# Attention on one Trainium2 core: a new order for the row-maximum pieces and later places for six products with V

## What is computed

```
h   = layernorm(x)
q, k, v = split(clip(h @ Wqkv.T, -8, 8))          # 512 columns each
q, k = layernorm(q) * q_w + q_b, layernorm(k) * k_w + k_b
scores = q k^T / 4 + alibi(head)                  # 32 heads of 16, causal
x   = x + softmax(scores) @ v @ Wout.T
W_q = sum over 4 of alphas * bases                # 512 x 512
x   = x + layernorm(x) @ W_q.T
```

## Time and profile before

| | |
|---|---|
| median of 3 runs | 701.35 us |
| profiled execution | 701.69 us, its span 700.0 us |
| mean granted TensorE clock | 0.973 of full |
| busy: PE, DVE, ACT, POOL | 673.8, 576.4, 410.5, 313.1 us |
| reductions of maximum pieces (L979) | 608, 358.3 us busy |
| exponentials (L806) | 640, 309.3 us busy |
| products with V (L1161) | 1536 passes, 156.8 us busy |

### The profile page before, as it was taken

The page is one execution under the profiler, slowest core; times in us unless marked ns, Lnnn a source line. Parts: engine busy times, 40 slices in busy tenths (PEclk is TensorE's granted clock), DMA queues, the critical chain, the costliest instruction groups (busy, mean ns, idle before and its releaser), DMA issues.

```text
span 700.0 us, 16007 instructions
## 1 busy us (share of the span) xinstructions
PE 673.8 (96%) x6096; PEld 412.5 (59%) x6096; DVE 576.4 (82%) x990; ACT 410.5 (59%) x855; POOL 313.1 (45%) x403
## 2 busy tenths in 40 slices
PE   3999999998899999999999999999999999899998
PEld 2888888885334554554554455445455543588886
DVE  6899999997999999989999998999999830466664
ACT  5133333232059887888888888888878889222221
POOL 1378666778132642634625523322322535234440
PEclk9999999998569999999999999999999999999999
DMA  8226665868926443343343434334333332245442
GB/s 307 69 68 181 181 181 155 224 174 225 300 89 167 126 134 98 106 128 101 115 124 101 115 109 130 97 113 124 106 113 117 95 92 73 75 135 154 144 131 75
DMA packets 102060, 93.64 MB, mean 134 GB/s; under 512 B 11640, under 2 KB 81912, under 8 KB 101984
## 3 DMA queue, kind: packets, MB, share of 16 engines
q1 hardware_dynamic: 97856, 86.84, 42.4%
q10 hardware_dynamic: 2016, 3.67, 2.0%
q0 software_dynamic: 2112, 2.10, 1.3%
HBM read 57.44 MB, written 33.82 MB: 130 GB/s over the span
## 4 chain that ended last, share of the span: by engine, by line
PE 72%; DVE 16%; issue 7%; DMA 2%; ACT 1%; POOL 1%; SPq 0%; DVEq 0%; POOLq 0%; ACTq 0%
PE ps L1126 23%; PE ps L1161 21%; PE ps L1106 9%; PE ps L1040 5%; PE ps L1041 5%; PE ps L1042 5%; DVE stats L979 4%; DVE qk_stat L924 2%; DVE qk L920 2%; PE ps L1048 2%; PE ps L1102 2%; DVE x_stat L890 1%; DVE xt_lo L883 1%; DMA inv_in<-inv_dram 1%; DVE rest L899 1%
## 5 line engine op out<-in xcount | busy, mean ns | idle before, releaser
L979 DVE TENSOR_REDUCE stats<-ps 128x1 f32<-128x512 f32 (+3 forms) x608 | 358.3, 656 | 31.6 <-PE ps L1106 29.3
L806 ACT ACTIVATE probs<-ps 128x512 f32<-128x512 f32 (+2 forms) x640 | 309.3, 560 | 71.3 <-PE ps L1126 70.9
L1106 PE MATMUL ps<-first_k,first_q 54*128 54x128 bf16 (+3 forms) x1152 | 217.3, 282 | 5.2 <-DVE stats L979 4.7
L1126 PE MATMUL ps<-second_q,second_k 64*128 64x128 bf16 (+4 forms) x1152 | 205.0, 273 | 0.0
L1126 PE MATMUL ps<-first_q,first_k 54*128 54x512 bf16 (+3 forms) x768 | 194.2, 328 | 0.2 <-ACT probs L806 0.2
L1161 PE MATMUL ps<-probs,v_sb 128*32 128x512 f32 (+3 forms) x1536 | 156.8, 496 | 2.0 <-ACT o_sb L837 1.2
L694 POOL TENSOR_SCALAR_AFFINE_SELECT probs<-probs 128x256 f32<-128x256 f32 x256 | 103.0, 408 | 123.7 <-ACT probs L806 116.6
L1126 PEld LDWEIGHTS ps<-first_q,first_k 54*128 54x128 bf16 x768 | 57.7, 94 | 111.1 <-ACT probs L806 108.3
L1106 PEld LDWEIGHTS ps<-first_k,first_q 54*128 54x128 bf16 x1152 | 92.3, 96 | 50.9 <-DVE stats L979 35.9
L1126 PEld LDWEIGHTS ps<-second_q,second_k 50*128 50x128 bf16 (+1 forms) x1152 | 91.8, 95 | 20.9 <-issue 0.6
L1040 PE MATMUL ps<-wqkv_hi,xt_hi 128*128 128x512 f32 x192 | 76.8, 400 | 0.0
(11 more groups left out here) (79 smaller groups left out, 822.7 us busy)
## 6 DMA issues: line engine op xcount, KB each, us to landing
parts_dram<-parts SPq DMA_DIRECT2D x48, 256.0 KB, 4.1
v_dram<-v_ext SPq DMA_DIRECT2D x16, 512.0 KB, 4.0
v_sb<-v_dram SPq DMA_DIRECT2D x16, 512.0 KB, 4.4
o_dram<-o_sb SPq DMA_DIRECT2D x32, 256.0 KB
first_q<-parts_dram SPq DMA_DIRECT2D x96, 64.0 KB
first_k<-parts_dram SPq DMA_DIRECT2D x96, 64.0 KB
second_q<-parts_dram SPq DMA_DIRECT2D x96, 64.0 KB
second_k<-parts_dram SPq DMA_DIRECT2D x96, 64.0 KB
```

The lines of the kernel that those rows point to most:

```text
L806: act.activation(weights, scores, ACT.Exp, scale=SCALE).then_inc(exp_done, 1)
L979: dve.tensor_reduce(to, scores, AX.X, ALU.max).then_inc(max_taken, 1)
L1106: last = pe.matmul(ps[:, bank, r * cols:(r + 1) * cols], first_q[n % STACKS][rows, hp, i * P:(i + 1) * P], first_k[n % STACKS][rows, hp, k ...
L1126: return pe.matmul(ps[:, bank, r * cols + first:r * cols + last], stack_k[n % STACKS][rows, heads[r] // PAIR, kb * P:(kb + 1) * P], stack_ ...
```

## The change

The order of the pieces is written out as a list, `PIECE_AT`, in place of `piece_plan`, and the step after which each product with V is due as a list, `WEIGH_AT`, in place of the unit's end. Numbers in `WEIGH_AT` are 6 less than the step at whose end the product stands.

```diff
+WEIGH_AT = [3, 8, 11, 11, 16, 21, 25, 29, 32, 35, 39, 39]
...
-PLAN = piece_plan()
+PIECE_AT = [15, 18, 6, 7, 14, 6, 9, 16, 17, 8, 7, 9, 2, 14, 1, 11, 10, 5, 13, 10,
+            5, 13, 18, 17, 4, None, 8, 2, 12, 1, 3, 15, 11, 4, 16, 12, 0, 0, None, 3]
+PLAN = [[] if m is None else [(m, (v + 1) % PAIR)] for v, m in enumerate(PIECE_AT)]
...
-                    if 0 <= e < GROUPS * NE and e % NE == UNIT_END[u]:
+                    if 0 <= e < GROUPS * NE and e % NE == WEIGH_AT[u]:
                         copy_half(e // NE, half, u)
...
-                    u = ENTRIES[e % NE][0]
-                    if e % NE == UNIT_END[u] and u + 1 not in NARROWEST:
-                        if u in NARROWEST:
-                            weigh(e // NE * NU + u - 1)
-                        weigh(e // NE * NU + u)
+                    for u in range(NU):
+                        if e % NE == WEIGH_AT[u]:
+                            weigh(e // NE * NU + u)
```

More of the change, by code:

```diff
@@ L88 @@
 UNIT_END = [max(k for k in range(NE) if ENTRIES[k][0] == u) for u in range(NU)]
-NARROWEST = [u for u in range(NU) if unit_columns(u)[1] == P]
 EXP_RING = 4
@@ L133 @@
 STATS = 3
[L136 to L148, removed]
-PLAN = piece_plan()
+PIECE_AT = [15, 18, 6, 7, 14, 6, 9, 16, 17, 8, 7, 9, 2, 14, 1, 11, 10, 5, 13, 10,
+            5, 13, 18, 17, 4, None, 8, 2, 12, 1, 3, 15, 11, 4, 16, 12, 0, 0, None, 3]
+assert [sorted(m for m in PIECE_AT[half::PAIR] if m is not None) for half in range(PAIR)] == [list(range(NM))] * PAIR
+PLAN = [[] if m is None else [(m, (v + 1) % PAIR)] for v, m in enumerate(PIECE_AT)]
 TAKES = [take for step in PLAN for take in step]
```

## The result

The changed kernel takes 691.99 us (median of 4 runs, 691.15 to 693.19) against 701.25 us for the kernel before beside it; the ratio is 0.9871, 95% interval 0.9860 to 0.9883. It is 9.3 us faster; 12.4 were forecast. The profiled execution has a span of 691.5 us against 700.0.

The account below looks back on a forecast made before the run. Neither TensorE nor VectorE alone was the bound: they block each other through three maximum banks. 13 x 0.86 = 11.2 us, plus 0.86 and 0.4 for the last and first intervals, gave 12.5: 701.35 to 688.9 us; range 673 to 702.

Parts of the forecast that it names:

- The period: Time from one row-maximum join to the next, per group of four heads: 22.06 us of VectorE work plus 1.89 lost, 23.95.
- the loop: From the third-last reduction ahead of a product with V to the first behind it: taken as 2.05 us, 1.85 for narrow ones.
- loop less cover: VectorE's loss at each product: that time minus the reductions still queued in the maximum banks; 1.89 us a group in all.
- TensorE's sum: TensorE's own work per group, added from steps, diagonals, products with V and transpose: 22.5 us, the higher floor.
- The waits of the weight loads for ACT: TensorE's weight loads idle 6.7 us a group because four score banks are full; should fall by about what is saved.
- The rule that VectorE's pitch alone counts: From a skill page on PSUM evacuation: only VectorE's reductions bound a group, saving 2.75 us each, 661 us; chance 0.03.
- Floor reached: Rival: even load lets the rings hide nearly all, period 22.5 to 23.2 us; at 22.8, 672 us; chance 0.17.
- Slower: Rival: TensorE isn't ahead at the products because new blocks have three steps; 0.82 us more lost per group, 713 us; chance 0.12.
- Clock: Rival: gaps on TensorE bring one 34 us half-clock stretch into the groups, costing about 14 us, 702 us; chance 0.03.
- either way: The first group's pieces, ahead of all scores, run without gaps at half clock and cost nothing in either order.
- The shift rows: Their last pair lands by 421.3 us, ahead of the reduction at 423.10; with over a microsecond of cover, costed at nothing.
- My sign for being wrong in kind: Waits for the shift rows or for o_sb appearing in the changed kernel's profile; no size given.

Follow-up runs that it names:

- the order alone: The changed kernel's new order of pieces, with the products with V left where they were in the kernel before: 711.6 us, ratio 1.0145.
- short reductions: Each maximum reduction reads only the first three quarters of its columns: 684.8 us on the changed kernel, 691.6 us on the kernel before.
- the places alone: The kernel before, its old order of pieces kept, with the six products with V moved later: 702.9 us, ratio 1.0030.
- the pairs apart: The changed kernel with two diagonal pieces swapped with plain ones, so no pair of diagonals stands right ahead of a product: 695.7 us, ratio 0.9921.
- the mixture: The changed kernel's new order of pieces with only products 4 and 5 moved to their new places: 704.8 us, ratio 1.0049.
- the masks issued twice: The two mask products of each diagonal piece issued twice: 718.5 us on the changed kernel, 727.7 us on the kernel before.
- the three products together: The changed kernel with products 1, 2 and 3 together at the end of step 15: 691.3 us with three-quarter reductions; 696.4 us with full ones and first group's old order.

## Why the prediction came out, and where its reasons failed

**The period.** I forecast joins 23.95 us apart and they are 24.02; the saving per group was 0.86 forecast and 0.80 measured. That is less merit than it looks, and in good part luck. The step "I take 2.05" for the loop stood for a mechanism, loop less cover on VectorE, that the runs don't bear out: with the same way of counting, the order alone should have made 693 to 697 us and made 711.6. What VectorE loses is not a cause of its own. In steady state its gaps must add up to the period less 22.06, whoever sets the period; with short reductions its idle time grows from 1.25 us a group (24.02 - 22.77) to 5.39 (23.88 - 18.49) and nothing gets slower.

**TensorE's sum** of 22.5 us was the term that was mis-sized: it is about 23.9 in the changed kernel (short reductions, 23.87) and 24.3 in the one before. The products were right. The steps were not: I had 40 x 0.33 + 1.04 - 1.1 = 13.1 us, and from the end of a product to the start of the next the ten stretches of a group add up to 14.5 us in the changed kernel with short reductions. The largest missing part is the change of the array's shape. TensorE in the changed kernel, around product 6:

```profile
413.42 0.39 PE L1116 MATMUL ps<-second_q,second_k 64*128 64x128 bf16 x2
413.74 1.07 PE L1151 MATMUL ps<-probs,v_sb 128*32 128x512 f32 x8
414.74 0.33 PE L1116 MATMUL ps<-first_q,first_k 54*128 54x384 bf16 x1
```

The two second products (128 and 384 columns) started at 413.42 are streamed by 413.42 + 512 / 2400 = 413.63, and the product starts at 413.74: 0.11 us of nothing. I had timed a product from its own start to the next and so left this out. Read in this way it is 0.09 to 0.11 us ahead of each of the ten products of this group, 1.0 us in all. The Trainium skill, page TensorEngine Tiling (Array Packing), section Key Properties, states that changing the tiling mode drains TensorE; the trace agrees, with this 0.11 us going in. What the remaining 0.4 us are, no run shows.

**The waits of the weight loads for ACT**, 6.7 us a group in the earlier trace rows, I read as full score banks. They are not. In the kernel before all ten of a group stand ahead of the first weight load behind a product: six of 0.84 us behind the wide ones, four of 0.20 to 0.63 behind the narrow ones. They last while the product streams (417.90 to 418.89 in the order-only kernel). They fell only to 6.2 us, where I had said that they would fall by what is saved; of these, 0.15 and 0.36 us stand away from the products, in the score steps, and there too a matmul still streams for nearly all of the wait. This misreading hid that TensorE was near its bound.

**Where the gain came from.** 0.37 of 0.80 us is TensorE waiting less for maximum banks: the change made the pieces evener for VectorE, as I said, with less than half of the size. The 0.42 us that stay with VectorE out of the way I had not foreseen. They lie between the products: with short reductions these stretches add up to 14.92 us a group before and 14.51 after, the products and the transpose to 9.37 and 9.36.

One part of it is plain to see, and I had overlooked it. The transpose stands at the start of step 28. Before, product 5 ends step 25, and the transpose stands alone among steps of 64-row products, with a change of shape of its own ahead of it:

```profile
415.35 0.38 PE L1106 MATMUL ps<-first_k,first_q 54*128 54x512 bf16 x1
415.66 0.28 PE L1175 MATMUL ps<-ident,peak 128*32 128x128 f32 x1
415.88 0.39 PE L1126 MATMUL ps<-first_q,first_k 54*128 54x512 bf16 x1
```

The piece is streamed by 415.35 + 0.21 = 415.56, so 0.10 us are without a stream. After, product 5 ends step 27 and the transpose follows it at once:

```profile
411.02 1.06 PE L1151 MATMUL ps<-probs,v_sb 128*32 128x512 f32 x8
412.02 0.28 PE L1165 MATMUL ps<-ident,peak 128*32 128x128 f32 x1
412.23 0.39 PE L1116 MATMUL ps<-first_q,first_k 54*128 54x512 bf16 x1
```

The product takes its usual 1.00 us and the transpose its 0.21. That is one such gap less a group, 0.1 us. Moving the transpose alone was not tried.

A count gives another 0.1 us. Between two products TensorE works off score products and pieces in two halves of 64 rows, which can stream side by side. If they always did, such a block would last as long as its fuller half. The score of step k lies in one half and its piece in the other; a diagonal piece has 1024 columns, with its masks. Steps 15 to 17 after the change have one half with two scores and one piece, 2 x 1024 + 512 = 2560 columns, and one with one score, a plain and a diagonal piece, 1024 + 512 + 1024 = 2560. With the old places steps 14 to 17 would have 3584 against 3072. Summed over the ten blocks the fuller half has 12.59 us of columns before, 12.48 after, 13.07 with the order alone, 12.80 with the places alone and 12.85 with the pairs apart (table).

This count was made after the runs, and they bear it out only in part. It puts the changed kernel, pairs apart and order alone in the order measured. But the mixture and pairs apart have the same 12.85 us and joins 25.03 and 24.23 us apart. And it fails at the masks issued twice: it gives 0.85 us a group more before and 1.07 after, and measured were 1.67 and 1.59. So the halves do not simply run side by side, least of all at diagonal pieces. TensorE's program is in order, and the second score product of a step stands behind the piece; whether that is the reason was not tested. The count accounts for 0.11 of the 0.42 us and the transpose for 0.1; what makes up the other 0.2 is open, and with it why order and places each alone lose.

**Rivals and costs at nothing.** *Floor reached*: it is, in effect, TensorE's floor, but at 23.9 and not at 22.8. The rule that VectorE's pitch alone counts (22.06 us a group, 661 us) did not hold: with VectorE's work cut by a quarter the period moved by 0.15 us. *Slower* did not come, though its place was near: the order-only and places-only kernels show that one part without the other costs 1.7 to 10.4 us. *Clock*: nothing fell in the groups (1.00 throughout); but the pieces of the first group at half clock, which I priced at nothing "either way", cost 0.76 us to the first join, and the interval behind it, where I had forecast 0.4 us less, took 0.3 us more. Against the forecast 0.8 us are missing in the 13 intervals, 0.7 in the first one, 1.8 ahead of it (1.0 of these before any piece) and 0.7 behind the last join; the timed medians differ by 0.8 us more than the two profiles. That makes the 3 us. The shift rows cost nothing, as said. My sign for being wrong in kind, a wait for o_sb, does appear in the changed kernel, 0.2 us a group, but under it TensorE has no longer gap than ahead of the other products; it was a cost only where product 4 kept its old place.

## What to carry to other kernels

Where two engines take turns, the idle time on one side is not the loss; shorten one side's instruction by a quarter in a trial and see whether the period moves. In this kernel it moved by 0.5 us before and 0.15 after, which says in one run each how much hangs on VectorE. An order of pieces and the places of the blocks between them are one decision, not two: each alone lost, together they won 1.3%. What needs the array in the same shape belongs side by side, as the transpose and a product here, but that has to be tried: the three products together lost. And an order tuned for the steady state may be kept out of the lead-in: leaving the first group in the old order gave another 2.5 us, 1.8 of them between runs of the same mean clock.

## What the runs showed of the hardware

Going from products on 64-row halves to products on 32-column strips left TensorE without a stream for 0.11 us (413.63 to 413.74), and for 0.10 us ahead of a transpose that stood alone (415.56 to 415.66). Putting two such products together shortened them (1.43 us against 2 x 0.79) and yet cost more than it saved: 24.25 against 23.87 us a group with short reductions, 24.50 against 24.02 with full ones. Extra matmuls of 64 rows at the diagonal pieces, as many on the upper half of the array as on the lower, showed at 93% and 98% of their streaming time one after the other (1.59 and 1.67 of 1.71 us); side by side they would have taken 0.85 and 1.07.
